# First group of a graph-and-convolution layer: h by graphs and the messages ahead of the first sub-convolution

## What is computed

```
h      = relu(layernorm(x))
c      = relu(bn1(conv1_1x1(h^T)))
x_conv = relu(bn2(conv2_17taps(c)) + h^T)^T
s      = h @ w_se.T + b_se                       # 3 numbers a node
A      = exp(-dist(s, s)) * adj
msg    = relu(h @ w_msg.T + b_msg)
x_nmp  = A @ msg                                 # per graph
gi, gh = [x_conv, x_nmp] @ w_ih.T + b_ih,  h @ w_hh.T + b_hh
r, z   = sigmoid(gi_r + gh_r), sigmoid(gi_z + gh_z)
out    = x + (1 - z) * tanh(gi_n + r * gh_n) + z * h
```

## Time and profile before

| | us |
|---|---|
| median of 3 runs | 280.0 |
| lowest, highest | 279.77, 280.37 |
| the profiled execution | 280.33 |
| its span, first to last instruction | 278.5 |
| TensorE busy | 271.4 (97%) |
| VectorE busy | 243.7 (87%) |
| ScalarE busy | 163.4 (59%) |
| GpSimd busy | 65.3 (23%) |

### The profile page before, as it was taken

How to read it: one execution, slowest core, us unless ns; L and a number is a source line. 1 busy time by engine, 2 the same in 40 slices (tenths; PEclk the granted TensorE clock), 3 DMA queues, 4 the chain that set the end, 5 groups by cost and what they waited for, 6 DMA issues and landing times.

```text
span 278.5 us, 5224 instructions
## 1 busy us (share of the span) xinstructions
PE 271.4 (97%) x1800; PEld 245.9 (88%) x1800; DVE 243.7 (87%) x550; ACT 163.4 (59%) x275; POOL 65.3 (23%) x127
## 2 busy tenths in 40 slices
PE   7999999999999999999999999999999999999993
PEld 6699978999889988899889998899889998899883
DVE  6899999898999889987999989987999887984666
ACT  3787469737753677517754567527674276541563
POOL 7900022720234002610216002530016100340000
PEclk9999999999999999999999999999999999999999
DMA  7950413654244545173532635363440604053002
GB/s 238 353 64 0 160 69 151 227 63 166 79 152 61 139 155 183 45 100 100 225 154 43 117 119 171 132 94 107 151 153 10 108 11 151 2 62 60 2 0 75
DMA packets 20797, 31.00 MB, mean 111 GB/s; under 512 B 9778, under 2 KB 14644, under 8 KB 19892
## 3 DMA queue, kind: packets, MB, share of 16 engines
q1 hardware_dynamic: 17552, 26.47, 28.4%
q0 software_dynamic: 3072, 4.20, 11.3%
q10 hardware_dynamic: 148, 0.01, 0.0%
HBM read 25.64 MB, written 8.70 MB: 123 GB/s over the span
## 4 chain that ended last, share of the span: by engine, by line
PE 93%; DMA 2%; DVE 2%; ACT 2%; issue 1%; DVEq 0%; ACTq 0%
PE ps L1348 24%; PE ps L1350 24%; PE ps L1349 24%; PE ps L1416 5%; PE ps L1459 5%; PE ps L1641 3%; DMA aff<-x_nm 2%; PE ps L1491 2%; PE ps L1482 2%; PE ps L1488 2%; PE ps L1437 1%; PE ps L1368 1%; ACT cp L559 1%; PE ps L1427 0%; DVE gn L1144 0%
## 5 line engine op out<-in xcount | busy, mean ns | idle before, releaser
L1348 PE MATMUL ps<-v_hi,wt_hi 128*128 128x256 f32 x280 | 78.8, 281 | 0.0
L1350 PE MATMUL ps<-v_hi,wt_lo 128*128 128x256 f32 x280 | 78.8, 281 | 0.0
L1349 PE MATMUL ps<-v_lo,wt_hi 128*128 128x256 f32 x280 | 78.6, 281 | 0.0
L1348 PEld LDWEIGHTS ps<-v_hi,wt_hi 128*128 128x128 f32 x280 | 52.7, 188 | 0.9 <-ACT msg L614 0.4
L1349 PEld LDWEIGHTS ps<-v_lo,wt_hi 128*128 128x128 f32 x280 | 52.7, 188 | 0.5
L1350 PEld LDWEIGHTS ps<-v_hi,wt_lo 128*128 128x128 f32 x280 | 52.6, 188 | 0.0
L427 POOL TENSOR_TENSOR scale<-vpe,neg_half 128x8 f32<-128x8 f32 x6 | 10.6, 1758 | 83.2 <-DVE scale L868 83.2
L596 ACT ACTIVATE mbs<-ps,par 128x256 f32<-128x256 f32 x24 | 12.1, 502 | 29.8 <-DVE y L998 17.6
L1348 PE MATMUL ps<-h_hi,wt_hi 128*128 128x512 f32 (+1 forms) x65 | 25.8, 398 | 0.5 <-ACT gate L692 0.4
L1350 PE MATMUL ps<-h_hi,wt_lo 128*128 128x512 f32 (+1 forms) x65 | 25.0, 384 | 0.0
L1349 PE MATMUL ps<-h_lo,wt_hi 128*128 128x512 f32 (+1 forms) x65 | 24.9, 384 | 0.0
(11 more groups left out here) (186 smaller groups left out, 640.1 us busy)
## 6 DMA issues: line engine op xcount, KB each, us to landing
w<-ln_rows SPq DMA_DIRECT2D x6, 1024.0 KB, 4.8
mask<-adj_t SPq DMA_DIRECT2D x8, 512.0 KB, 3.3
out<-x_t SPq DMA_DIRECT2D x7, 512.0 KB, 5.3
out<-gate POOLq DMA_DIRECT2D x14, 256.0 KB, 4.1
xt<-x_t SPq DMA_DIRECT2D x6, 512.0 KB, 3.6
xin<-x_nm SPq DMA_DIRECT2D x5, 512.0 KB, 5.2
slot_rows<-turned SPq DMA_DIRECT2D x24, 32.0 KB, 3.1
rows<-slot_rows SPq DMA_DIRECT2D x6, 128.0 KB, 2.5
```

Source lines behind the costliest of these rows:

```text
L1348: pe.matmul(dst, wt_hi[:, blk, :], hi, start=start, stop=False)
L1349: pe.matmul(dst, wt_hi[:, blk, :], lo, start=False, stop=False)
L1350: return pe.matmul(dst, wt_lo[:, blk, :], hi, start=False, stop=stop)
```

## The change

On TensorE the messages of group 0 stand ahead of the first sub-convolution, in the place of two idle matmuls, and don't wait for c. On ScalarE one copy by graphs stands ahead of each half of cp; lot 1 follows cp; the reads of the messages come between v_hi from vtb and lot 4; hf comes later; v_hi from vtu stands ahead of lots 7 to 10; and in the seam all four of ScalarE's normalized tiles come behind `update_rows`. On VectorE the lots and v's levels change places. The bias rows land in y, and the wait for their split moves to y's first writer.

```diff
-        row_raw = hg[0:33].rearrange("p b n -> p (b n)")[:, 0:3 * MW]
+        row_raw = y[0:33, 0:3 * MW]
...
@@ scalar @@
             h_rows_first()
-            lot_high(1)
             act.wait_ge(pool_par, 5)
             act.wait_ge(pads_set, 2)
+            act.wait_ge(h_lo_ready, 1)
+            by_graphs(0, 0, 6)
             conv1_rows(0, 0, 0)
+            act.wait_ge(h_lo_ready, 2)
+            by_graphs(0, 1, 7)
             conv1_rows(0, 1, 2)
+            lot_high(1)
             lot_high(2)
             act.wait_ge(pads_set, 6)
-            hf_rows_first()
             lot_high(3)
             v_high_b(0, 1)
+            messages(0, 3)
             lot_high(4)
-            act.wait_ge(row_split, 3)
-            by_graphs(0, 0, 6)
-            by_graphs(0, 1, 7)
+            hf_rows_first()
             lot_high(5)
             v_high_u(0, 0)
             m_shared(0, 0)
-            for n in range(6, 11):
+            lot_high(6)
+            v_high_u(0, 1)
+            for n in range(7, 11):
                 lot_high(n)
-            v_high_u(0, 1)
-            messages(0, 3)
             slots_first(1)
...
             reset_rows(0, 0)
-            ln_rows_first(1, (4, 5))
             update_rows(0, 0)
-            ln_rows_first(1, (6, 7))
+            ln_rows_first(1, range(4, GB))
             candidate(0, 0)
@@ vector @@
             def add_h(g):
+                if g == 0:
+                    dve.wait_ge(row_split, 3)
                 dve.wait_ge(mb_ready, 2 * g + 2)
...
             lot_low(2)
+            v_low_b(0, 1)
             lot_low(3)
-            v_low_b(0, 1)
+            level1(0)
             lot_low(4)
-            level1(0)
+            v_low_u(0, 0)
+            level2_u(0)
             lot_low(5)
-            v_low_u(0, 0)
             join_b(0, 0)
+            v_low_u(0, 1)
             lot_low(6)
-            level2_u(0)
             lot_low(7)
-            v_low_u(0, 1)
             join_b(0, 1)
@@ tensor @@
             def messages(g, first=0):
-                pe.wait_ge(c_ready, NCH * g + (NCH if g > BY_TRANSPOSE + 1 else 1))
+                if g:
+                    pe.wait_ge(c_ready, NCH * g + (NCH if g > BY_TRANSPOSE + 1 else 1))
                 pe.wait_ge(hg_ready, NCH * g + NCH)
...
             message_biases(3)
-            keep_busy(2)
+            messages(0, 3)
             sub_conv_first(0)
             sub_conv_first(1)
             sub_conv_first(2)
-            messages(0, 3)
             sub_conv_first(3)

```

## The result

| | before | changed |
|---|---|---|
| median, us | 280.02 (19 runs) | 280.72 (19 runs) |
| the profiled execution, us | 280.33 | 280.61 |
| its span, us | 278.5 | 278.8 |

The ratio is 1.0024, with an interval of 1.0013 to 1.0035: the changed kernel is slower by 0.7 us. The forecast was 280.9, in a range of 279.5 to 281.4.

What follows compares the result with a forecast made beforehand. TensorE never lacks input after about 45 us, so passing the seam decides, with VectorE as full. Convolution 1 of group 1 0.80 later plus 0.1 restart gives +0.9 on 280.0: 280.9 us, range 279.5 to 281.4.

Steps and rivals of the forecast that it cites:

- Part 1: TensorE, first group: removed idle matmuls worth nothing; message matmuls, 1.71 us, fall into the wait before the first sub-convolution.
- Part 2: ScalarE up to cp: second copy not hidden; messages' 1.71 us free, fourth sub-convolution could start 1.3 us earlier.
- c_ready is 0.48 later: ScalarE at cp's second half: the second copy by graphs delays c, and VectorE's queue with it, by 0.48 us.
- Part 3: ScalarE from 14.4 us: with 1.37 us of message reads ahead, v_hi from u 0.71 later; 0.7 of 1.3 us left.
- Part 4: VectorE up to the seam 1.1 us later; TensorE waits 0.8 for lot 5, eighth sub-convolution 0.82 later.
- the second 0.6: VectorE: lot 5's low part behind v_lo and level 2 adds 0.60 us; without it 1.1 falls to 0.5, no change.
- Part 5: Seam: aff issued 0.82 later, landing 5.58 after issue; convolution 1 of group 1 0.80 later, plus 0.1 restart: +0.9 us.
- VectorE's queue decides: Seam, lower end: aff lands sooner after its issue, stats at 38.96 and not 39.13, total +0.7 us.
- The seam edit: ScalarE's tiles behind update_rows: TensorE's 0.4 us gate wait goes, but TensorE arrives 0.5 earlier at convolution 1 and waits there.
- A: Rival, join of y: TensorE's queue alone decides, y not late; 279.3 us, or 278.8 with the seam's 0.5; chance 0.12.
- B: Rival, seam: gate wait returns 0.5, VectorE catches up before aff lands, h_lo not last; +0.3, 280.3 us; chance 0.18.
- C: Rival, seam: transfers collide more, +1.2 or, with a longer wait for mbs0, +1.4; 281.2 to 281.4 us; chance 0.10.

Runs made afterwards that it cites:

- experiment 1: Kernel before with only the seam edit: ScalarE's four normalized tiles all behind update_rows; 280.29 against 280.03 us, ratio 1.0008.
- 2: Changed kernel without the seam edit, ScalarE's tiles before and behind update_rows as in the kernel before; 280.98 us, 1.0032 of before.
- Experiment 5: Changed kernel with ScalarE's message reads moved behind v_hi from u and mbs0; 280.40 us, 1.0011 of before.
- experiment 4: Changed kernel with lot 5's low part ahead of v_low_u(0, 0) on VectorE, level 2 left in place; 280.60 us, 1.0021 of before.
- experiment 3: Changed kernel with VectorE's level2_u(0) moved ahead of v_low_u(0, 0), into its idle time; 280.52 us, 1.0013 of before.
- 7: Kernel of experiment 3 with VectorE's statistics of aff moved behind the normalized tiles; 279.81 us, 0.9983 of before.
- 11: Kernel of 7 with GpSimd's rstd of group 1 cut into two halves, VectorE's tiles behind the first; 279.47 against 280.15 us, 0.9975.
- experiment 12: Kernel before with the edits of experiment 1, 6 and 11 at the seam and nothing else; 279.51 against 279.98 us, 0.9987.
- 6: Kernel before with only VectorE's statistics of aff moved behind the normalized tiles; 279.84 against 280.07 us, 0.9992.
- 9: Kernel of 7 with ScalarE's message reads also moved behind m_shared(0, 0); 280.18 against 280.15 us, 0.9998.
- experiment 10: Kernel of 7 with only the low parts of lots 11 and 12 (the gates) moved from VectorE to GpSimd; 280.78 us, 1.0032 of before.
- experiment 8: Kernel of 7 with the low parts of lots 8 to 12 moved from VectorE to GpSimd; 283.03 us, 1.0101 of before.

## Why the prediction was right, and where it was not

**What bounds, and where to look: right.** From 46 us on the kernels run alike (TensorE is busy 228.13 and 228.39 us of the 232 from 46 to 278). The lag of 0.44 us at 45 us is still 0.26 at 98 us and 0.28 at the end; where the rest goes I did not follow.

**Part 1: right.** The messages start at 11.75 and are hidden; nothing waits for them.

**Part 2: right in its order, its term too large.** "c_ready is 0.48 later" took the whole second copy as added. Of two executions that start alike (experiments 1 and 2) VectorE gets c only 0.24 later. In experiment 1 the halves of cp start at 10.40 and 11.24, 0.84 us apart, where they follow each other after 0.68 in the trace of before (10.71 and 11.39): a part of the copy falls into that gap. The rows of before come from the one execution with a late start (9.37), and no step of mine allowed for another. This quarter of a microsecond runs on through parts 3 and 4.

**Part 3: right, and shown.** v_hi from u was forecast at 18.35 and stands at 18.08, 3.92 us behind v_hi from vtb, for 3.91 in the sum. The fourth sub-convolution was forecast at 19.5 and stands at 19.34. Experiment 5 takes ScalarE's 1.37 us from in front of it and wins some 0.6 back on VectorE.

**Part 4: the waits are right, the size a quarter too large, and the cause incomplete.** At the join of y VectorE is 0.83 late, or 0.85 of two that start alike, for 1.1 forecast; TensorE's eighth sub-convolution 0.63 or 0.65, for 0.82; it waits 0.60 at 21.38 for lot 5, for 0.8. Nearly all of the difference is the 0.24 of part 2. But the sentence that lot 5's place carries the second 0.6, and that the loss would fall to 0.5 without it, was wrong: experiment 4 moves the lot and gains 0.1. Only with level 2 in the idle time (experiment 3) is VectorE back at its old place. I had counted the idle time of one queue and not asked which of the rows behind it has a second engine waiting.

**Part 5: the step that failed.** "Lands 5.58 us later" was taken as a length that moves with the issue. It isn't one. Issue and landing of aff in all fourteen profiled executions (the landing is the issue and the time to landing):

| kernel | issue | landing | us |
|---|---|---|---|
| 3 | 32.40 | 38.84 | 6.4 |
| 7 | 32.46 | 39.0 | 6.6 |
| 11 | 32.56 | 38.6 | 6.0 |
| 1 | 32.59 | 38.26 | 5.7 |
| 5 | 32.60 | 38.38 | 5.8 |
| 12 | 32.67 | 38.1 | 5.4 |
| 6 | 32.70 | 38.4 | 5.7 |
| before | 32.71 | 38.29 | 5.6 |
| 9 | 32.78 | 39.0 | 6.2 |
| 2 | 33.19 | 38.3 | 5.1 |
| 4 | 33.21 | 38.3 | 5.1 |
| changed | 33.30 | 38.2 | 4.9 |
| 10 | 33.62 | 38.9 | 5.3 |
| 8 | 36.12 | 41.5 | 5.4 |

From 32.4 to 33.6 us the landing doesn't follow the issue: it lies between 38.1 and 39.0, in no order of the issues. Issued 2.5 us later still (8), it lands 2.6 us later. What holds the landing was not tried on its own and stays open. The changed kernel's aff was therefore not late. VectorE's queue and GpSimd's rstd were: forecast 39.13 for the statistics and 45.37 for convolution 1 of group 1, measured 38.52 and 45.01. Of the 0.74 us by which VectorE was late at xc_lo, 0.46 are left at nmr (39.56 against 39.10) and 0.44 at convolution 1, where the forecast had 0.80: before's seam is held by the landing, the changed kernel's is not, and between the two some 0.3 are given back. The medians show +0.7 for +0.9, the lower end which the prediction gave for "VectorE's queue decides"; but the trace accounts for 0.44 of it only, so that the median came so near the forecast is in part luck. The estimate from the Trainium skill ("DMA: Bandwidth & Descriptors", anatomy of one DMA, which is written for transfers issued by GpSimd; this one is SyncE's) led to that same end, but not for its reason: it makes 3.4 us of what takes 4.9 to 6.6 here.

**The seam edit: right.** Worth nothing in experiments 1 and 2, for the reason given: the gate's wait goes and h_lo's takes its place.

**The rivals.** A (the lead is kept) failed at the join of y, where the prediction put its test. B (the lag is given back at the seam) was so for 0.3 of 0.74 us in the trace, as told under part 5, but h_lo was still the last to arrive. The same seam took in the traces the whole gain of 3 (0.90 us at the join of y) and half of that of 5 (0.71), which the prediction, looking only at a lag, did not see. C did not happen.

## What to carry to other kernels

Before a row is moved past a wait on an in-order engine, list what stands behind the wait and send first what another engine has to answer; a result that only the last consumer reads can come after. Where a gain upstream disappears at a join, look at all that arrives there within half a microsecond: here the transfer, the statistics, GpSimd's rstd and h_lo lay so close that neither edit tried alone (1 and 6) gave anything clear of noise, and the three of experiment 12 together gave 0.4 to 0.5 us. Filling a busy engine's idle time is worth something only if the other full queue gets shorter: the messages in TensorE's wait gave 0.9 us at the fourth sub-convolution, and with or without them the mended kernel takes 279.5 us.

## What the runs showed of the hardware

- VectorE's instructions with two inputs in SBUF and GpSimd's subtractions exclude each other for whole instructions: 0.17 us became 0.88 to 1.24 (experiment 8), 0.68 became 1.73 (experiment 10). Moving 1.34 us of such work from VectorE to GpSimd took the kernel from 0.9983 to 1.0032 of before. GpSimd's power didn't stretch VectorE's xc_lo beside it (0.69), and itself took 0.3 to 0.4 us longer there.
- After 2.5 us without work TensorE's granted clock was 0.54 from 27.3 to 31.0 us, and 3.61 us went into work that otherwise takes 1.94 (experiment 8).
- A transfer's time from issue to landing can't simply be added to a moved issue: the same 512 KB took 4.9 to 6.6 us, the longest where it was issued earliest.
- Fourteen idle matmuls of 128x512 took 5.09 to 5.79 us at the start in two executions, with a granted clock of 1.00 from 3 to 8 us in both. It moved the start of convolution 1 by 0.2 us, and of this little was left at the seam. What decides it stays open.
